# First cross-attention: turned scores of two key blocks at a time, kept in their banks by key differences

## Chip, cores and metric

The kernel runs on one core of a Trainium2 chip. The metric is the device time of one execution in microseconds (us), the median of several runs; smaller is better. Matmuls run on TensorE (PE in the profile, its weight loads on the row PEld), the other engines are VectorE (DVE), ScalarE (ACT), GpSimd (POOL) and SyncE (SP), which issues most DMAs. PSUM has eight banks of 128x512 float32 that matmuls write to; one bank holds one 512-column result.

## What is computed

The program is a two-layer decoder for 4 batches of 256 tokens and 256 channels. The change is inside the first layer's cross-attention alone. Its scores are 256 queries times 1601 keys for each of 16 heads and 4 batches; keys and values of a batch are the same 1601x64 array for all heads once the per-head matrices are folded into the queries:

```python
kv_r = _apply_rope(kv_c, sin_k[None], cos_k[None])
q_r = jnp.einsum('bshq,hqr->bhsr', q_big, W_qr)
k_r = jnp.einsum('bld,hdr->bhlr', kv_r, W_kr)
scores = jnp.einsum('bhsr,bhlr->bhsl', q_r, k_r)
attn = jax.nn.softmax(scores, axis=-1)
ctx_c = jnp.einsum('bhsl,bld->bhsd', attn, kv_r)
```

Before it stand the first layer's recurrent attention and the query products, after it the experts and the second layer; of these the change touches only what borders on the stage.

## The kernel before

The stage is a loop over 32 units (`UNITS = B * PAIRS`): a unit is one batch b and one pair p of heads. `QALL` holds the queries turned, split into a high part of reduced precision (fp32r) and the rest: for head h of the pair, rows 64h to 64h+63 hold the high part and the other 64 rows the low part. The keys of a batch lie turned in `KH` (high part, the same 64 rows twice, one above the other) and `KL` (low part). The 1601 keys make 13 blocks of 128, the last of 65.

A unit has four kinds of PE work. **Plain scores** (`plain_scores`, six per unit, and `plain_tail` for the last 65 keys): high parts only, queries on PSUM's partitions, two heads at once on the upper and lower 64 rows of the array, 2x512 columns into two banks. DVE takes their row maxima (`maxima`, L1620; `tail_maxima`, L1628; `all_maxima`, L1636), PE turns the four columns of maxima into rows (`turn_maxima`, L728), and DVE spreads these rows into rows 64 to 67 of `QM` (`maximum_rows`, L1644). **Turned scores** (`turned_scores`): keys on the partitions, for each of the 13 blocks one matmul `KH` with all 128 rows of `QALL` and one `KL` with `QM` (64 rows of high parts and the four maxima), 512 columns each, so that the bank holds score minus maximum. ACT writes its exponential into `PWS` (`weights`, L1277). **Context** (`context`): 13 blocks of weights times the values `KVR`, in float32, both heads side by side on the array's columns, into bank 7. **Weight sums** (`weight_sums`, of the unit before): POOL adds up the weights (`added_up`: five adds of 128x1024, L2075, one of 128x512, L2079, one of 65x512, L2082), PE sums over the partitions, DVE inverts the sums, multiplies the context and splits it (`normalised`, L1653 and L1657, `low_part`, L1663; `high_part` on ACT, L1288).

PSUM: banks 0 to 2 go round (`st_bank`) among turned blocks, tails, turned maxima, turned keys of the next batch and sums; banks 3 to 6 are two pairs for the plain scores (`plain_banks`). Plain scores run a unit ahead of their use. Every engine runs its own list in order; a `wait_ge` holds the engine's next instruction and all behind it. In 12 of the units PE also turns a quarter of the next batch's keys (`keys`, L684), ACT copies them out and DVE subtracts. All matmuls of the stage but the turns carry line L515, that of the helper `mm`.

The order of PE within a unit: the first six turned blocks, the tail of the next unit, two plain scores, the other seven blocks, two plain scores, the turn of the next maxima, keys if due, the sums of the unit before, the 13 context blocks, two plain scores.

Of the kernel before, what the change touches and what calls it, by code (L numbers as in the profile page):

```python
# [13 lines left out]
P = 128  # L14
# [13 lines left out]
HALF = 512  # L28
# [6 lines left out]
QW = 192  # L35
E0, E1 = 8, 16
# [50 lines left out]
def decoder(nc, x, ctx_512, L0_attn_Wk, L0_attn_Wv, L0_attn_Wr, L0_attn_Wo, L0_attn_time_decay, L0_attn_time_first,  # L87
# [5 lines left out]
    with ExitStack() as ctx:  # L93
# [75 lines left out]
        KH = [at("KH0", 65536, [P, L + 1], F32R), at("KH1", 78400, [P, L + 1], F32R)]  # L169
        KL = [at("KL0", 71968, [P, L + 1], F32R), at("KL1", 145152, [P, L + 1], F32R)]  # L170
        PWS = at("PWS", 104480, [P, 15 * HALF])
        PW = [PWS[:, 2 * HALF * c:2 * HALF * (c + 1)] for c in range(6)] + [PWS[:, 14 * HALF:15 * HALF]]
        ACC = PWS[:, 12 * HALF:14 * HALF]
        QM = [at(f"QM{i}", 135200 + 2048 * i, [P, HALF], F32R) for i in range(2)]
        WS = [at(f"WS{i}", 139296 + 2048 * i, [P, HALF]) for i in range(2)]
        pm = [at(f"pm{i}", 143392 + 128 * i, [P, 2, 2, 4]) for i in range(2)]
        nm = [at(f"nm{i}", 143456 + 32 * i, [P, 4]) for i in range(2)]
# [208 lines left out]
        kl_ready = sem("key_low_parts")  # L386
# [40 lines left out]
        CHUNKS = 7  # L427
        PLAINS = 6
        ADDS = 7
        FRONT, BACK = range(0, 6), range(6, LT)  # L430
# [12 lines left out]
        def keys_due(u):  # L443

            b, p = divmod(u, PAIRS)
            return (b + 1, p // 2) if p % 2 == 0 and b < B - 1 else None

        AHEAD = 4

        def plains_after(u):  # L450

            return [[n for n in range(PLAINS * (u + 1) + a, PLAINS * (u + 1) + z) if n < PLAINS * UNITS]
                    for a, z in ((4, 6), (6, 8), (8, 10))]

        ST_ITEMS = [("tail", 0), ("maxima", 0)]
        for u in range(UNITS):
            ST_ITEMS += [("block", LT * u + lt) for lt in (FRONT if u else range(LT))]
            ST_ITEMS += [("tail", u + 1)] if u + 1 < UNITS else []
            ST_ITEMS += [("block", LT * u + lt) for lt in (BACK if u else ())]
            ST_ITEMS += [("maxima", u + 1)] if u + 1 < UNITS else []  # L460
            ST_ITEMS += [("keys", *keys_due(u))] if keys_due(u) else []
# [4 lines left out]
        def st_bank(*item):  # L466

            n = ST_AT[item] % 3
            return PS[:, n * 512:(n + 1) * 512]

        def plain_banks(n):

            return PS[:, (3 + 2 * (n % 2)) * 512:(5 + 2 * (n % 2)) * 512]

        def st_freed(n):

            kind, *at_ = ST_ITEMS[n]
            return {"keys": lambda: (kl_ready, 4 * (at_[0] - 1) + at_[1] + 1), "maxima": lambda: (qm_ready, at_[0] + 1),
                    "block": lambda: (p_ready, at_[0] + 1), "tail": lambda: (tail_read, at_[0] + 1),
                    "sums": lambda: (norm_done, at_[0] + 1)}[kind]()  # L480
# [26 lines left out]
        def _(pe):  # L507
# [143 lines left out]
            def first_keys():  # L651

                pe.wait_ge(dup_ready, 2)
                for q in range(4):
                    ps = begin(("k", q), "dve")
# [3 lines left out]
                    last.then_inc(filled, 1)  # L659

            wait_ht(1)
            banks.start_at(4)
# [15 lines left out]
            def keys(b, q):  # L678

                pe.wait_ge(dup_ready, 2 * (b + 1))  # L680
                ps = st_begin("keys", b, q)
# [5 lines left out]
            def plain_scores(n):  # L687

                u, i = divmod(n, PLAINS)
# [4 lines left out]
                if n == 1:  # L694
                    pe.wait_ge(*banks.emptied(("q", PAIRS - 1, 0)))
                if n >= 2:
                    pe.wait_ge(nat_read, n - 1)
                if p == 0 and b > 0:
                    pe.wait_ge(kl_ready, 4 * (b - 1) + i % 3 + 1)
                for h in range(2):  # L700
                    st, k0 = i // 3, i % 3 * HALF
                    last = mm(plain_banks(n)[:, h * 512:(h + 1) * 512], QALL[h * D:(h + 1) * D, p, b, h, st * P:(st + 1) * P],
# [3 lines left out]
            def plain_tail(u):  # L706

                b, p = divmod(u, PAIRS)
                if u == 0:
                    pe.wait_ge(*banks.emptied(("q", PAIRS - 1, 1)))  # L710
                    pe.wait_ge(rows_set, 1)
                    for s in range(2):
                        pe.wait_ge(q_moved[s], 32 * PAIRS)
                ps = st_begin("tail", u)
                if p == 0 and b > 0:
                    pe.wait_ge(rows_set, 2)
                    pe.wait_ge(kl_ready, 4 * b)
                for h in range(2):
                    for st in range(2):
                        a = h * 256 + st * P  # L720
                        last = mm(ps[:, a:a + 66], QALL[:, p, b, h, st * P:(st + 1) * P], KH[b % 2][:, 3 * HALF:3 * HALF + 66])
                last.then_inc(tail_full, 1)

            def turn_maxima(u):

                pe.wait_ge(mx_ready, u + 1)
                ps = st_begin("maxima", u)
                nc.tensor.transpose(ps[0:4, 0:P], nm[u % 2][:, :], ident[:, :]).then_inc(mt_full, 1)  # L728

            def turned_scores(u, blocks):  # L730

                b, p = divmod(u, PAIRS)
                if blocks is FRONT:
                    pe.wait_ge(qh_moved[u % 2], 32 * (u // 2 + 1))
                    pe.wait_ge(qm_ready, u + 1)
                for lt in blocks:
                    w = P if lt < LT - 1 else LREST + 1
                    ps = st_begin("block", LT * u + lt)[0:w, :]
                    mm(ps, KH[b % 2][:, lt * P:lt * P + w], QALL[:, p, b, :, :], True, False)
# [1637 lines left out]
```

## Time and profile before

| | us |
|---|---|
| median of 3 runs (1345.43 to 1349.94) | 1347.24 |
| the profiled execution | 1343.5 |
| its span, first to last instruction | 1341.7 |
| PE busy in the span | 1241.2 (93%) |
| DVE, ACT, POOL busy | 890.9, 630.1, 821.2 |
| cross-attention loop, first plain score to last context (193.46 to 710.83) | 517.4 |

The span is read in stretches: the loop of 32 units lies between 193.46 and 710.83 us. A timeline row gives start, duration, engine, line, operation, output<-inputs, shape and count; durations of matmuls are modelled ends of pipelined instructions, so the step from one start to the next tells what a matmul costs, and the duration does not. In brackets stands how long the engine had been idle and what released it.

### The profile page before, as it was taken

The page shows a single profiled execution, that of the slowest core. Times are in us where ns is not written, and L with a number is a line of the kernel's source. Part 1 is how long each engine was busy: PE and PEld are TensorE (multiplying, and loading weights), DVE is VectorE, ACT ScalarE, POOL GpSimd, SP SyncE. Part 2 cuts the span into 40 slices and gives each one's busy share as a digit, 9 for nine tenths or more (in the row PEclk, how much of TensorE's full clock was granted, in tenths as well). Part 3 has the DMA queues.
Part 4 walks back from the last instruction along what each step waited for, and adds up shares of the span by engine and source line. Part 5 has one row for each costly group of instructions (what it writes and reads, how often), then busy time and mean ns, then how long its engine had stood idle before and what let it go on. Part 6 is the DMA issues. An engine that isn't in the chain of part 4 may idle for free.

```text
span 1341.7 us, 20371 instructions
## 1 busy us (share of the span) xinstructions
PE 1241.2 (93%) x7123; PEld 811.9 (61%) x7123; DVE 890.9 (66%) x1522; ACT 630.1 (47%) x1669; POOL 821.2 (61%) x747
## 2 busy tenths in 40 slices
PE   7999988999999999999999758998999998998992
PEld 4865545666666666666668644444777785557682
DVE  4789995777777777778865636766666213664643
ACT  3721123544445455444551514887766124882251
POOL 1267005999999999999993444888544002661354
PEclk9989998999999999999999787999999999999997
DMA  9501110000000000000005620000000105200273
GB/s 268 138 9 40 40 40 12 9 13 9 9 9 9 9 9 13 9 8 9 9 5 181 196 67 6 1 1 1 1 1 1 29 0 159 64 2 33 63 158 117
DMA packets 66172, 58.91 MB, mean 44 GB/s; under 512 B 19424, under 2 KB 62968, under 8 KB 65560
## 3 DMA queue, kind: packets, MB, share of 16 engines
q1 hardware_dynamic: 62952, 49.09, 13.1%
q0 software_dynamic: 3120, 8.52, 2.8%
q8 instruction: 58, 0.95, 0.3%
q14 instruction: 42, 0.34, 0.1%
HBM read 40.69 MB, written 8.52 MB: 37 GB/s over the span
## 4 chain that ended last, share of the span: by engine, by line
PE 78%; DVE 6%; ACT 6%; POOL 5%; issue 3%; DMA 2%; DVEq 0%; POOLq 0%; SPq 0%; ACTq 0%
PE PS L515 72%; PE PS L523 5%; ACT s_sc L1393 2%; POOL a_m L2132 2%; POOL a_m L2126 2%; DVE s_mx L1857 2%; ACT a_m L1347 1%; POOL e_yg L2180 1%; DVE pm L1620 1%; DVE HN L1495 1%; PE PS L728 0%; DVE stats L1485 0%; DMA f_xg<-token_rows,f_ids 0%; POOL s_sc L2147 0%; ACT PWS L1277 0%
## 5 line engine op out<-in xcount | busy, mean ns | idle before, releaser
L2075 POOL TENSOR_TENSOR PWS<-PWS 128x1024 f32<-128x1024 f32 x160 | 379.5, 2372 | 43.1 <-ACT PWS L1277 23.7
L1620 DVE TENSOR_REDUCE pm<-PS 128x2 f32<-128x1024 f32 x192 | 225.9, 1219 | 65.9 <-PE PS L515 65.2
L1277 ACT ACTIVATE PWS<-PS 128x512 f32<-128x512 f32 (+1 forms) x416 | 212.7, 600 | 76.7 <-PE PS L515 75.2
L515 PE MATMUL PS<-PWS,KVR 128*64 128x256 f32 (+1 forms) x1664 | 186.2, 380 | 0.0
L515 PE MATMUL PS<-QALL,KH 128*128 128x512 f32 (+1 forms) x416 | 181.7, 437 | 0.9 <-DVE QM L1644 0.9
L515 PE MATMUL PS<-QM,KL 68*128 68x512 f32 (+1 forms) x416 | 166.0, 399 | 0.0
L2147 POOL TENSOR_SCALAR s_sc<-s_sc,s_ri 128x128 f32<-128x128 f32 (+1 forms) x256 | 103.9, 425 | 92.4 <-DVE s_ri L1864 92.4
L515 PEld LDWEIGHTS PS<-PWS,KVR 128*64 128x64 f32 (+1 forms) x1664 | 122.0, 138 | 58.7 <-issue 1.1
L515 PEld LDWEIGHTS PS<-QALL,KH 128*128 128x128 f32 (+1 forms) x416 | 77.2, 186 | 77.1 <-ACT PWS L1277 57.4
L1393 ACT ACTIVATE s_sc<-PS,s_nb 128x128 f32<-128x128 f32 (+1 forms) x256 | 104.3, 432 | 4.5 <-DVE s_nb L1860 4.5
L1857 DVE TENSOR_REDUCE s_mx<-PS 128x2 f32<-128x512 f32 (+2 forms) x112 | 65.7, 611 | 45.5 <-PE PS L515 45.4
L515 PE MATMUL PS<-KH,QALL 64*128 64x512 f32 (+1 forms) x512 | 88.7, 406 | 6.9 <-DVE pm L1620 6.9
L515 PE MATMUL PS<-a_wT,HT 128*128 128x512 f32 x192 | 93.6, 621 | 0.7 <-issue 0.7
L1288 ACT ACTIVATE QALL<-CTX 128x256 fp32r<-128x256 f32 x32 | 13.3, 417 | 154.3 <-DVE CTX L1657 154.3
L515 PEld LDWEIGHTS PS<-QM,KL 68*128 68x128 f32 (+1 forms) x416 | 78.3, 188 | 5.8
L515 PEld LDWEIGHTS PS<-KH,QALL 64*128 64x128 f32 (+1 forms) x512 | 46.7, 187 | 43.4 <-issue 25.8
L2126 POOL TENSOR_TENSOR a_m<-a_m,a_m 128x512 f32<-128x512 f32 x40 | 50.8, 1270 | 29.6 <-DVE a_m L1834 29.6
L1516 DVE TENSOR_TENSOR X<-X,PS 128x256 f32<-128x256 f32 x40 | 16.7, 419 | 76.6 <-PE PS L515 76.6
L515 PE MATMUL PS<-z_HTh,z_w 128*128 128x512 f32 x192 | 65.7, 412 | 1.8 <-DVEq L502 1.8
L1262 ACT ACTIVATE QALL<-PS 64x512 fp32r<-64x512 f32 x32 | 18.9, 592 | 94.8 <-PE PS L515 94.4
L2175 POOL DMA_INDIRECT e_x<-token_rows,e_ids x31 | 29.4, 949 | 54.5 <-DVE e_ids L1954 44.5
L1653 DVE RECIPROCAL PS<-PS 128x256 f32<-128x256 f32 x32 | 55.9, 1747 | 6.6 <-PE PS L515 6.6
(333 smaller groups left out, 2487.3 us busy)
## 6 DMA issues: line engine op xcount, KB each, us to landing
QALL<-qlo SPq DMA_DIRECT2D x32, 128.0 KB, 2.4
QM<-QALL SPq DMA_DIRECT2D x64, 64.0 KB, 2.0
f_w<-in_L_ffn_w_dram SPq DMA_DIRECT2D x2, 2048.0 KB, 16.4
tile_results<-e_y SPq DMA_DIRECT2D x31, 128.0 KB, 2.5
a_nat<-in_L_attn_w_qkv_dram SPq DMA_DIRECT2D x1, 3072.0 KB, 12.7
x_wq<-in_L_xattn_Wq_dram SPq DMA_DIRECT2D x1, 2048.0 KB, 10.9
x_wo<-in_L_xattn_Wo_dram SPq DMA_DIRECT2D x2, 1024.0 KB, 7.3
a_wo<-in_L_attn_w_o_dram SPq DMA_DIRECT2D x1, 2048.0 KB, 17.2
```

The lines of the kernel that those rows point to most:

```text
L515: return nc.tensor.matmul(o, a, b, start=start, stop=stop, **kw)
L523: last = nc.tensor.transpose(ps[0:w, c:c + r], a, ident[0:r, 0:r])
L1277: nc.scalar.activation(PW[c][0:rows, j * HALF:(j + 1) * HALF], st_bank("block", LT * u + lt)[0:rows, :], ACT.Exp).then_inc(p_ready, 1)
L1393: ins = nc.scalar.activation(s_sc[:, k % 4, h, 0:nk], ps[:, j * nk:(j + 1) * nk], ACT.Exp, bias=s_nb[:, k % 3, h:h + 1], scale=scale, accu ...
L1620: V.tensor_reduce(pm[u % 2][:, :, i // 3, i % 3], src, AX, ALU.max).then_inc(nat_read, 1)
L1653: V.reciprocal(sums, sums).then_inc(inv_ready, 1)
L1857: ins = V.tensor_reduce(s_mx[:, k % 3, i * per:(i + 1) * per], banks.bank(key)[:, 0:per * nk].rearrange("p (h k) -> p h k", h=per), AX, AL ...
L2075: G.tensor_tensor(ACC[:, :], PW[0][:, :] if i == 0 else ACC[:, :], PW[i + 1][:, :], ALU.add).then_inc(acc_step, 1)
L2126: G.tensor_tensor(a_m1[:, n % 6, :], a_m1[:, n % 6, :], a_m2[:, n % 2, :], ALU.add).then_inc(m_sum, 1)
L2132: G.tensor_tensor(m1, m1, a_bt[:, i, s, :].unsqueeze(1).to_broadcast([P, 4, P]), ALU.add).then_inc(qk_ready, 1)
L2147: ins = G.tensor_scalar(s_sc[:, n % 4, h, 0:nk], s_sc[:, n % 4, h, 0:nk], s_ri[:, n % 4, h:h + 1], 1.0, ALU.mult, ALU.mult)
L2175: G.indirect_dma_start(e_x[:, j % 8, :], None, xs1, IndirectOffsetOnAxis(ap=e_ids[:, j:j + 1], axis=0)).then_inc(tile_back[j % 8], 16)
```

## The change

Turned scores are now taken for two key blocks at a time (`turned_pair`): block 2j on the upper 64 rows of the array, block 2j+1 on the lower 64, each into a bank of its own. So a unit has seven parts (`PARTS = 7`), six of two whole blocks and one of the last 65 keys. Because 64 rows hold only one part of a query, each product is made in steps: the key's high part with `QALL` (512 columns), with `QS`, a copy of the queries with halves swapped (512 columns), and the key's low part with each head's high part (256 columns each). The last part splits its two heads over the halves instead of two blocks.

The maxima are no longer added to every block. `max_rows` writes them at the start of a unit into the four banks 0 to 3 (part j uses banks 0 and 1 or 2 and 3), and each part adds onto what its banks hold. From part 2 on, the stationary operand is not the keys of a block but their difference to the block four earlier, so that the bank moves from one score to the next. These differences are made once per batch on POOL (`PD`, in `doubled`), turned, and split into `KDH` and `KDL`. `KH` stays for the plain scores, `KL` goes.

With this the banks are dealt out anew: one pair (4 and 5) for the plain scores instead of two, one bank (6) for turned maxima, keys and sums in turn instead of three that go round, banks 2 and 3 also for the tails. ACT takes two banks in one exponential of 128x1024, seven per unit for thirteen. The context comes in three parts between the others, and plain scores are spread singly. POOL's add of 128x512 goes; PE's weight sums have two steps of accumulation for one. `normalised` writes into bank 6 and `high_part` and `low_part` read it there, one unit later. Keys are due in 18 units instead of 12: four of each batch turn whole keys (ACT copies), two turn differences (ACT copies, DVE subtracts). SP copies 128 KB twice per unit into `QS`, for 64 KB twice into `QM`.

The core of the diff, PE's side first:

```diff
+        ST_BANK = PS[:, 6 * 512:7 * 512]
+        PLAIN_BANKS = PS[:, 4 * 512:6 * 512]
+        TAIL_BANKS = PS[:, 2 * 512:4 * 512]
...
+        def pair_banks(j):
+            return PS[:, 2 * (j % 2) * 512:2 * (j % 2 + 1) * 512]
...
             def st_begin(*item):
                 n = ST_AT[item]
-                if n >= 3:
-                    pe.wait_ge(*st_freed(n - 3))
-                return st_bank(*item)
+                if n >= 1:
+                    pe.wait_ge(*st_freed(n - 1))
+                return ST_BANK
...
-                if n >= 2:
-                    pe.wait_ge(nat_read, n - 1)
+                else:
+                    pe.wait_ge(nat_read, n)
...
+            def max_rows(u, j):
+                pe.wait_ge(qm_ready, u + 1)
+                if u > 0:
+                    pe.wait_ge(p_ready, PARTS * (u - 1) + PARTS - j)
+                if j == 1:
+                    pe.wait_ge(tail_read, min(u + 2, UNITS))
+                for s in range(2):
+                    rows = slice(s * D, (s + 1) * D)
+                    mm(pair_banks(j)[:, s * 512:(s + 1) * 512], ones_r[rows, :], MX[rows, :], True, False,
+                       skip_group_check=True)
+
+            def turned_pair(u, j):
...
+                if j >= 2:
+                    pe.wait_ge(p_ready, PARTS * u + j - 1)
...
+                    for q in (QALL[:, p, b, :, :], QS[u % 2]):
+                        for s, rows in enumerate(halves):
+                            mm(both[:, s * 512:(s + 1) * 512], KDH[b % 2][rows, cols], q[rows, :, :], False, False,
+                               skip_group_check=True)
+                    for h in range(2):
+                        for s, rows in enumerate(halves):
+                            q = QALL[rows, p, b, h, :] if s == h else QS[u % 2][rows, h, :]
+                            last = mm(both[:, s * 512 + h * T:s * 512 + (h + 1) * T], KDL[b % 2][rows, cols], q, False, True,
+                                      skip_group_check=True)
...
             for u in range(UNITS):
+                spots = plains_of(u)
+                plain_scores(spots[0])
                 if u + 1 < UNITS:
                     plain_tail(u + 1)
+                max_rows(u, 0)
+                turned_pair(u, 0)
+                max_rows(u, 1)
+                turned_pair(u, 1)
+                plain_scores(spots[1])
+                context(u, (0, 1))
+                plain_scores(spots[2])
+                turned_pair(u, 2)
+                turned_pair(u, 3)
+                plain_scores(spots[3])
+                context(u, (2, 3))
+                plain_scores(spots[4])
+                turned_pair(u, 4)
+                turned_pair(u, 5)
+                plain_scores(spots[5])
+                turned_pair(u, 6)
                 if u + 1 < UNITS:
                     turn_maxima(u + 1)
                 if keys_due(u):
                     keys(*keys_due(u))
                 if u >= 1:
                     weight_sums(u - 1)
-                context(u, range(LT))
+                context(u, (4, 5, 6))
```

DVE's list of a unit and ACT's exponentials:

```diff
             for u in range(UNITS):
+                spots = plains_of(u)
                 if u + 1 < UNITS:
                     tail_maxima(u + 1)
+                for n in spots[0:4]:
                     maxima(n)
                 if u + 1 < UNITS:
                     all_maxima(u + 1)
+                if u >= 2:
+                    low_part(u - 2)
+                for n in spots[4:6]:
                     maxima(n)
                 if u + 1 < UNITS:
                     maximum_rows(u + 1)
                 if keys_due(u):
                     keys(*keys_due(u))
...
+                if j < PARTS - 1:
+                    nc.scalar.activation(PW[j], pair_banks(j), ACT.Exp).then_inc(p_ready, 1)
```

## Rows read from the trace of the kernel before

**Rows 1.** Two whole units: us, busy us (instructions) of each engine, PEclk, DMA.

```profile
457.39:473.36 15.97, 15.97 (x106) 9.95 (x104) 11.32 (x14) 7.81 (x16) 14.98 (x8) 1.00 0.05 11
473.36:488.90 15.54, 15.54 (x103) 9.55 (x101) 12.62 (x13) 7.64 (x16) 14.67 (x8) 1.00 0.03 8
```

**Rows 2.** Chain of waits, 440 to 500 us: start, us, what carried the end.

```profile
456.98 15.32 PE PS L515 x98
```

**Rows 3.** Timeline of PE, 455 to 480 us.

```profile
456.91 0.65 PE L515 MATMUL PS<-WS,ones 128*64 128x256 f32 x4
457.39 5.78 PE L515 MATMUL PS<-PWS,KVR 128*64 128x256 f32 x52
463.11 0.73 PE L515 MATMUL PS<-KH,QALL 64*128 64x512 f32 x4
463.77 0.50 PE L515 MATMUL PS<-QALL,KH 128*128 128x512 f32 x1
464.11 0.39 PE L515 MATMUL PS<-QM,KL 68*128 68x512 f32 x1
...
468.54 0.40 PE L515 MATMUL PS<-QALL,KH 128*128 128x512 f32 x1
...
469.47 0.50 PE L515 MATMUL PS<-QALL,KH 128*128 128x512 f32 x1
...
472.34 0.60 PE L684 MATMUL PS<-ident,DUP 128*128 128x128 f32 x4
472.87 0.65 PE L515 MATMUL PS<-WS,ones 128*64 128x256 f32 x4
```

**Rows 4.** Timeline of PE's weight loads, 463.0 to 463.3 us.

```profile
463.11 0.30 PEld L515 LDWEIGHTS PS<-KH,QALL 64*128 64x128 f32 x4 [0.39 <-issue]
```

**Rows 5.** Timeline of PE, 712.0 to 712.45 us: 256 columns each, after the loop.

```profile
712.08 0.28 PE L515 MATMUL PS<-UL,QALL 128*128 128x256 f32 x1
...
712.43 0.28 PE L515 MATMUL PS<-UL,QALL 128*128 128x256 f32 x1
```

**Rows 6.** Timeline of POOL, 465 to 482 us.

```profile
467.79 12.44 POOL L2075 TENSOR_TENSOR PWS<-PWS 128x1024 f32<-128x1024 f32 x5
480.31 1.35 POOL L2079 TENSOR_TENSOR WS<-PWS 128x512 f32<-128x512 f32 x1
481.74 1.29 POOL L2082 TENSOR_TENSOR WS<-WS,PWS 65x512 f32<-65x512 f32 x1
```

**Rows 7.** Timeline of DVE, 455 to 480 us.

```profile
463.65 2.36 DVE L1620 TENSOR_REDUCE pm<-PS 128x2 f32<-128x1024 f32 x2 [0.96 <-PE PS L515]
467.41 0.43 DVE L1628 TENSOR_REDUCE pm<-PS 128x4 f32<-128x260 f32 x1 [1.40 <-PE PS L515]
...
470.24 0.17 DVE L1636 TENSOR_REDUCE nm<-pm 128x4 f32<-128x16 f32 x1
...
474.50 0.68 DVE L1644 TENSOR_TENSOR QM<-PS,ident 4x512 fp32r<-4x512 f32 x1
```

**Rows 8.** DVE's groups by form, 190 to 715 us: busy, mean ns, idle before.

```profile
L1663 DVE TENSOR_TENSOR CTXL<-CTX,QALL 128x256 fp32r<-128x256 f32 x31 | 45.4, 1465 | 15.0 <-ACT QALL L1288 15.0
...
L1657 DVE TENSOR_TENSOR CTX<-CTX,PS 128x256 f32<-128x256 f32 x31 | 13.0, 421 | 1.1
```

**Rows 9.** ACT's groups by form, whole span: busy, mean ns, idle before.

```profile
L1277 ACT ACTIVATE PWS<-PS 128x512 f32<-128x512 f32 x384 | 197.5, 601 | 76.7 <-PE PS L515 75.2 <-POOL WS L2079 1.0 <-issue 0.4
...
L1288 ACT ACTIVATE QALL<-CTX 128x256 fp32r<-128x256 f32 x32 | 13.3, 417 | 154.3 <-DVE CTX L1657 154.3
L1283 ACT ACTIVATE CTX<-PS 128x256 f32<-128x256 f32 x32 | 12.3, 384 | 35.5 <-PE PS L515 35.5
```

**Rows 10.** Timeline of ACT, 455 to 480 us.

```profile
464.62 3.08 ACT L1277 ACTIVATE PWS<-PS 128x512 f32<-128x512 f32 x6 [1.01 <-PE PS L515]
```

**Rows 11.** Timeline of PE's weight loads, 684 to 685 us: a load that waits.

```profile
684.70 0.19 PEld L515 LDWEIGHTS PS<-QALL,KH 128*128 128x128 f32 x1 [0.27 <-ACT PWS L1277]
```

**Rows 12.** DMA issues of the page: KB each, us to landing.

```profile
QALL<-qlo SPq DMA_DIRECT2D x32, 128.0 KB, 2.4
```

More of the change, by code:

```diff
@@ L35 @@
 QW = 192
+PARTS = 7
 E0, E1 = 8, 16
@@ L659, in first_keys, with turn_pairs @@
                     last.then_inc(filled, 1)
+                pe.wait_ge(dup_ready, 5)
+                for i in range(2):
+                    turn_pairs(begin(("paired", i), "dve"), 0, i).then_inc(filled, 1)
+            def turn_pairs(ps, b, i):
+                for n, j in enumerate(range(4 * i, min(4 * i + 4, PARTS))):
+                    w = P if j < PARTS - 1 else LREST
+                    last = nc.tensor.transpose(ps[:, n * P:n * P + w], PD[b][0:w, j, :], ident[0:w, 0:w])
+                return last
             wait_ht(1)
-            banks.start_at(4)
+            banks.start_at(2)
             z_jobs(0)
@@ new lines, in context @@
+            def context(u, chunks):
+                b = u // PAIRS
+                if chunks[0] == 0:
+                    pe.wait_ge(*((ctx_read, u) if u else banks.emptied(("q", PAIRS - 1, 1))))
+                for c in chunks:
+                    pe.wait_ge(p_ready, PARTS * u + c + 1)
+                    for j, lt in enumerate(range(2 * c, min(2 * c + 2, LT))):
+                        w = P if lt < LT - 1 else LREST
+                        for h in range(2):
+                            last = mm(CTX_BANK[h * D:(h + 1) * D, 0:T], KVR[0:w, b, lt, :],
+                                      PW[c][0:w, j * HALF + h * T:j * HALF + (h + 1) * T], lt == 0, lt == LT - 1)
+                    last.then_inc(ctx_part, 1)
@@ L760, in weight_sums @@
                 ps = st_begin("sums", u)
-                for h in range(2):
-                    last = mm(ps[h * D:(h + 1) * D, 0:T], ones[:, 0:D], WS[u % 2][:, h * T:(h + 1) * T])
+                for k in range(2):
+                    for h in range(2):
+                        last = mm(ps[h * D:(h + 1) * D, 0:T], ones[:, 0:D], ACC[u % 2][:, k * HALF + h * T:k * HALF + (h + 1) * T],
+                                  k == 0, k == 1)
                 last.then_inc(sum_full, 1)
@@ L1293, in _ @@
             for u in range(UNITS):
-                weights(u, FRONT)
-                weights(u, BACK)
+                for j in range(PARTS):
+                    weights(u, j)
+                    if j == 0 and u >= 2:
+                        high_part(u - 2)
                 if keys_due(u):
                     keys(*keys_due(u))
-                if u >= 1:
-                    high_part(u - 1)
                 if 0 <= u - SPLIT_FROM < PAIRS:
```

321 lines of the change are left out of this document (165 added, 156 removed).

## Prediction, made before the changed kernel ran

> **What bounds the kernel now.** Read two whole units in stretches first [rows 1]: one with a key step takes 15.97 us, one without 15.54. PE is busy for all of both, POOL for 14.98 and 14.67, DVE for 11.32 and 12.62, ACT for under 8, at a granted clock of 1.00 (2.4 GHz). The chain of waits [rows 2] stays on PE's matmuls for a unit at a time. So PE's own list sets the pace: nothing it asks for is late. POOL comes next: five adds take 12.52 from the first start to the start of the small add, which is 1.43 from the next [rows 6]; with two small adds that is 15.38, only 0.16 under PE. Twenty units without and twelve with keys make 20 x 15.54 + 12 x 15.97 = 502.4 us. The sum below is made against the profiled execution, 1343.5; the median of the runs, 1347.2, lies 3.7 above it, and I add that at the end. About 0.3% (4 us) is what a measurement of this kernel can tell from no change.
>
> **Prices on PE.** A matmul of 512 columns on the full array costs 0.232: four steps lie between 468.54 and 469.47 [rows 3]. Two matmuls on the upper and lower 64 rows run together: the plain scores do that now, and four of them, two pairs, take 0.66 from 463.11 to 463.77 [rows 3]. Two steps of 0.232 are 0.46; the other 0.20 is the price of changing the array's mode: about 0.1 of idling, and a first weight load that nothing hides (the first matmul of a run lasts 0.50, later ones 0.39). That the second pair's weights load beside the first pair shows in the four loads: they begin at 463.11 and have ended by 463.41 [rows 4]. So a pair costs what one full matmul costs, 0.232. For 256 columns the nearest rows are those after the loop, three steps in 0.35 or 0.117 each [rows 5]; I take 0.118 for a pair, with 0.232 as the upper end (weights that cost as much as in a 512-column step). A turn or a tail piece costs 0.11 to 0.13 (four turns in 0.53 with the change of mode, [rows 3]); two heads' context for a block 0.432 (13 in 5.72 with the change), the sums 0.48 with a change of mode of 0.05, so 0.43 for their two steps.
>
> **PE's work per unit after the change, waits apart.** Context 13 x 0.432 = 5.62. Plain scores 6 x 0.232 = 1.39. Tail, two pairs, 0.22. Maxima rows 2 x 0.232 = 0.46. Six parts of two 512- and two 256-column pairs, 6 x 0.70 = 4.20. The last part 3 x 0.118 = 0.35. Turn of maxima 0.11. Sums, now two steps of accumulation, 0.86. Changes of mode: three back to rows and one to the turn at 0.21, three to columns at 0.15: 1.29. Together 14.50, against 15.54: a gain of 1.04 per unit, of which the turned scores alone give 26 x 0.232 = 6.03 less 5.01. Key steps cost 0.43 in 18 units for 12 before.
>
> **What falls off the path.** POOL: five adds and one small one, 12.52 + 1.43 = 13.95, below PE. The differences for three batches (a copy of 256, subtractions of 512 and 128 columns, about 2.1 by the 1.35 of a 512-column add) fit into POOL's slack, and cost 2.1 each without it. ACT: six exponentials of 1024 columns, about 8 per unit in all. SP: two transfers of 128 KB land in about 2.4 [rows 12], queued a whole unit ahead; without that cover they would cost 2.4 per unit. DVE's total falls to about 11.3.
>
> **The new waits.** A walk through one unit in PE's order decides. Zero is the end of the previous context. Prices: from the issue of a first plain pair to DVE's start 0.54 (463.11 to 463.65, [rows 3, 7]), of which 0.11 is the weight load, 0.22 the stream, 0.22 the way; a reduction 1.18 to 1.22 (two in 2.36), I take 1.19; tail maxima 0.43, column maxima 0.17 and now twice, maxima rows 0.69 [rows 7]. From matmul to ACT likewise 0.22 to 0.28 (464.11 + 0.23 to 464.62, [rows 3, 10]). An exponential of 1024 columns is not in the trace: 512 take 0.601 and 256 columns 0.384 [rows 9], so 0.434 more, 1.0; ends are 0.87 (column time alone) and 1.2 (two of 512). ACT can start the next one 0.09 earlier (six in 3.08, [rows 10]). An engine's answer reaches PE 0.05 later.
> - PE: plain A at 0.21, tail, maxima rows, part 0 to 1.60, part 1 to 2.53. Plain B needs A reduced, because the pair of banks is now single: DVE has done the tail by 1.31 and A by 2.50; wait 0.13.
> - ACT: exponential 0 from 1.82 to 2.82, then the high part moved in between (0.42, [rows 9]), exponential 1 to 4.06. PE is at its context at 3.91: wait 0.25.
> - Plain C, parts 2 and 3, plain D at 6.86: C is reduced at 6.87, and the weights load exposed: wait 0.17. Context of parts 2 and 3 waits 0.07 and 0.05 for exponentials that end at 7.38 and 8.29.
> - Plain E at 9.47, parts 4 and 5, plain F: wait 0.17, issued at 11.16. Part 6 adds onto the banks of part 4, whose exponential ends at 11.62: wait 0.28, done at 12.13, then the turn of the maxima.
> - The sums use the same bank 6 as that turn, and wait until DVE has made the maxima rows from it. DVE takes its list in order: reduction of F from 11.72 to 12.91, rows to 13.60. PE could have started at 12.46 and starts at 13.65: **wait 1.19**. Behind the sums stand five context blocks and the whole next unit. Before, three banks went round and this answer had a context of 5.7 to hide in.
> - Sums and five blocks: the unit ends at 16.73, that is 14.50 and 2.3 of waits.
>
> In a key unit bank 6 is passed on once more: the keys wait for the maxima rows, the sums for ACT's copy of the keys (0.60): 1.41 more, 18.14, in 12 units. In the 6 that turn differences DVE's subtraction follows (0.69 and 0.05): 18.88. POOL and DVE have slack against such periods. `low_part` reads PSUM now: nearest is the other product with one PSUM operand, 0.42, and not the 1.47 with both operands in SBUF [rows 8]; were it 1.47, plain F would be later by half a us, 17 us in all.
>
> Sum: 14 x 16.73 + 12 x 18.14 + 6 x 18.88 = 565.2, against 502.4: **62.8 us more**. At the edges six first plain scores now follow one another at 1.8 rather than 1.19 (+3), seven more turns cost 0.8, unit 0 has no sums and unit 31 no maxima to wait for (-3); I count them as nothing, within 5. So 1343.5 + 62.8 = 1406.3, and by the median 1410.
>
> The bounds: four exponentials of the unit lie on its path, so 1.2 instead of 1.0 costs 0.8 per unit, 26 us, and 0.87 gives back 12. The 256-column pairs at 0.232 add 15 x 0.114 = 1.7 per unit, half of it inside waits: 27. The low part adds 17. Any one of the upper ends with the edges gives about 1441, the lower end 1388 to 1393.
>
> **Rivals.**
> 1. *PE goes past the held instruction* (faster). Place: the sums at bank 6. If only the waiting matmul were held and the five context blocks behind it ran, 2.2 of work would cover the 1.19, and the other waits would fill likewise. Price: -1.04 x 32 + 6 x 0.43 = -30.7, so 1316. It decides as soon as the waits of a unit stay under the gain of 1.04. For it: POOL's 13.95 would allow it. Against: a weight load that waits for ACT today leaves PEld idle for 0.27 although work for other banks stands behind it [rows 11]. 5%.
> 2. *Weights of a row half load only when that half is free.* Then nearly every pair bears a load of 0.107: some 26 per unit that are not exposed anyway, 2.8 x 32 = 89 more: 1499. The four loads of [rows 4] speak against it: two begin while the first pair runs. 5%. The Trainium skill, page "TensorE: Matmul & The Clock Gate", section "The mechanism", states that a weight load overlaps running matmuls only when its row group differs; by that rule this rival would be the forecast. The trace differs here: [rows 4] has loads for both row groups beside matmuls on both.
> 3. *The halves do not run together when they add onto banks* (the change doesn't do what it says). The plain scores start their banks anew, so no row shows it. Fourteen pairs of 512 and fifteen of 256 would double: 5.0 per unit, 161 us less at most 35 of waits hidden: about 1550. Against: matmuls that add cost the same 0.23 as those that start a bank [rows 3]. 2%.
> 4. *Half of the waits are covered* by something I can't see: they are 3.0 per unit on average, so 48 less: 1362. 5%. If two thirds were covered, no change: 3%.
>
> **How the numbers follow.** The forecast, waits as walked, 1410, has 80%, with its range 1388 to 1441. Rivals 2 and 3 (7%) lie above, 1 and 4 (13%) below, so that range leaves 20% out and stands. Faster by over 0.3%: 5%. Within: 3%. Slower: 92%.
>
> **What would show it.** In the trace after: PE idle before the sums, about 1.2 in plain units and twice that with keys, released by DVE's maxima rows or by ACT's copy of the keys; unit periods near 16.7, 18.1 and 18.9; pairs 0.232 apart and 0.118 for 256 columns; exponentials near 1.0; POOL idle for some 2.8 per unit, where it now idles for under one. If the periods lie under 15.7, the walk is wrong; if PE is busy throughout and slower, a price is.

## The result, and the profile after

The changed kernel takes 1424.46 us (median, 1421.91 to 1425.0); the kernel before took 1346.34 beside it. The ratio is 1.058 (95% interval 1.054 to 1.063): slower by 78 us, where 63 were forecast. The profiled execution took 1421.91 with a span of 1419.5. Its 78 us all lie in the loop of 32 units: from the start of the first plain score to the start of the last context matmul it takes 597.1 us now for 517.0 (the 517.4 of the table ahead goes to that matmul's end), 80 us more, and what lies around the loop is 2 us shorter. Loops are read between these two starts from here on.

From the page after: busy us, share and instructions of the engines, and the granted clock in 40 slices.

```profile
PE 1254.6 (88%) x8303; PEld 839.5 (59%) x8303; DVE 862.9 (61%) x1547; ACT 618.3 (44%) x1485; POOL 783.1 (55%) x731
PEclk9999979999999999999999978899999999999997
```

PE is busy for 88% now, 93% before. Its 1254.6 us are 13 more than before, and the other engines are busy for less: work did not grow by 78 us, something waits. Three units after, in stretches (us, busy us and instructions of PE, PEld, DVE, ACT, POOL, then PEclk, DMA share, GB/s): one without keys, then two with keys. They answer [rows 1].

```profile
342.27:359.17 16.90, 15.49 (x135) 10.30 (x136) 11.06 (x14) 6.96 (x10) 15.63 (x10) 1.00 0.08 17
359.18:379.16 19.98, 17.78 (x140) 11.70 (x140) 11.06 (x14) 7.55 (x11) 13.08 (x6) 0.91 0.06 14
379.16:397.46 18.30, 16.09 (x140) 10.71 (x140) 11.06 (x14) 7.55 (x11) 13.09 (x6) 1.00 0.07 15
```

The second and the third do the same work, and differ by 1.68 us and by the granted clock. Rows of PE's timeline of the unit without keys, from its third plain block on (start, duration, operation, output<-inputs, shape, count; in brackets the idle time and who ended it); it answers [rows 3]:

```profile
344.39 0.50 PE L513 MATMUL PS<-KH,QALL 64*128 64x512 f32 x2
344.72 0.39 PE L513 MATMUL PS<-QALL,KDH 64*128 64x512 f32 x2
344.95 0.40 PE L513 MATMUL PS<-QS,KDH 64*128 64x512 f32 x2
345.19 0.28 PE L513 MATMUL PS<-QALL,KDL 64*128 64x256 f32 x1
...
345.43 0.40 PE L513 MATMUL PS<-QALL,KDH 64*128 64x512 f32 x2
...
351.63 0.30 PE L745 MATMUL PS<-ident,nm 128*68 128x128 f32 x1
353.05 1.08 PE L513 MATMUL PS<-PWS,ones 128*64 128x256 f32 x8 [1.12 <-DVE MX L1715]
353.94 2.36 PE L513 MATMUL PS<-PWS,KVR 128*64 128x256 f32 x20
```

The reader sees the forecast's main wait: PE idles for 1.12 us between the turn of the maxima and the sums, until DVE has made the maxima rows (forecast 1.19). DVE's timeline shows why; it makes them only after the reduction of the sixth plain block:

```profile
351.09 1.23 DVE L1688 TENSOR_REDUCE pm<-PS 128x2 f32<-128x1024 f32 x1 [0.60 <-PE PS L513]
352.23 0.68 DVE L1715 TENSOR_TENSOR MX<-PS,spread 68x512 fp32r<-68x512 f32 x1
```

In a key unit bank 6 is passed on twice. PE's timeline in two key units, the first at full clock, the second (from 408.23) not; behind them the stretch from each unit's sums on:

```profile
389.93 0.63 PE L695 MATMUL PS<-ident,DUP 128*128 128x128 f32 x4 [1.14 <-DVE MX L1715]
391.34 1.08 PE L513 MATMUL PS<-PWS,ones 128*64 128x256 f32 x8 [0.78 <-ACT KH L1328]
...
408.23 0.63 PE L695 MATMUL PS<-ident,DUP 128*128 128x128 f32 x4 [1.14 <-DVE MX L1715]
409.64 1.83 PE L513 MATMUL PS<-ACC,ones 128*64 128x256 f32 x8 [0.78 <-ACT KH L1328]
```

```profile
391.34:394.50 3.16, 3.16 (x28) 2.27 (x28) 2.00 (x2) 0.00 (x0) 3.08 (x2) 1.00 0.00 0
409.60:412.90 3.30, 3.26 (x17) 2.32 (x19) 1.40 (x1) 0.00 (x0) 3.22 (x2) 0.53 0.00 0
```

The waits are the same. But in the second unit the sums take 1.83 instead of 1.08, at a granted clock of 0.53, that is at 1.2 GHz for nearly all of the stretch, in which PE gets through 17 matmuls where the first unit has 28. The record of the granted clock holds 11 such stretches of 3.41 us in the loop after its beginning, every one in a unit with keys; before, the loop had none after its beginning. That is the part of the loss that the forecast did not have.

### The profile page after: what moved, and what is told of

Same layout as the page of the kernel before. It is cut to its first block, busy times and chain, and to the rows that moved or that the text cites. A ratio compares the mean times of both kernels' runs of the same rounds, so it can differ in the third digit from the quotient of the medians.

```text
span 1419.5 us, 22602 instructions
## 1 busy us (share of the span) xinstructions
PE 1254.6 (88%) x8303; PEld 839.5 (59%) x8303; DVE 862.9 (61%) x1547; ACT 618.3 (44%) x1485; POOL 783.1 (55%) x731
## 4 chain that ended last, share of the span: by engine, by line
PE 71%; ACT 8%; DVE 7%; issue 6%; POOL 5%; DMA 2%; POOLq 0%; ACTq 0%; SPq 0%; DVEq 0%
PE PS L513 66%; PE PS L521 4%; ACT PWS L1339 3%; ACT s_sc L1458 2%; POOL a_m L2216 2%; DVE MX L1715 2%; POOL a_m L2210 1%; DVE s_mx L1930 1%; ACT a_m L1412 1%; POOL e_yg L2264 1%; DVE pm L1688 1%; DVE HN L1560 1%; PE PS L695 0%; DVE stats L1550 0%; DMA f_xg<-token_rows,f_ids 0%
## 5 line engine op out<-in xcount | busy, mean ns | idle before, releaser
L1339 ACT ACTIVATE PWS<-PS 128x1024 f32<-128x1024 f32 x192 | 189.9, 1024 | 209.2 <-PE PS L513 209.0
L2163 POOL TENSOR_TENSOR PWS<-PWS 128x1024 f32<-128x1024 f32 x80 | 189.2, 2365 | 82.9 <-ACT PWS L1339 75.8
L2163 POOL TENSOR_TENSOR ACC<-ACC,PWS 128x1024 f32<-128x1024 f32 x64 | 151.2, 2362 | 21.5 <-ACT PWS L1339 14.4
L513 PE MATMUL PS<-QALL,KDH 64*128 64x512 f32 (+1 forms) x448 | 87.2, 384 | 3.5 <-ACT PWS L1339 1.3
L513 PE MATMUL PS<-QALL,KDL 64*128 64x256 f32 (+1 forms) x448 | 85.9, 277 | 0.0
L513 PE MATMUL PS<-QS,KDH 64*128 64x512 f32 (+1 forms) x448 | 85.6, 376 | 0.0
L513 PEld LDWEIGHTS PS<-KH,QALL 64*128 64x128 f32 x512 | 46.8, 189 | 58.5 <-issue 35.8
L513 PEld LDWEIGHTS PS<-QALL,KDL 64*128 64x128 f32 (+1 forms) x448 | 75.4, 178 | 8.3
L513 PEld LDWEIGHTS PS<-QS,KDL 64*128 64x128 f32 x384 | 71.0, 185 | 8.1
L513 PE MATMUL PS<-QS,KDL 64*128 64x256 f32 x384 | 74.8, 278 | 0.0
```

The source lines that it names most:

```text
L513: return nc.tensor.matmul(o, a, b, start=start, stop=stop, **kw)
L1339: nc.scalar.activation(PW[j], pair_banks(j), ACT.Exp).then_inc(p_ready, 1)
L2163: G.tensor_tensor(acc, PW[0][:, :] if i == 0 else acc, PW[i + 1][:, :], ALU.add).then_inc(acc_step, 1)
```

## Experiments

Theory A: the waits around the shared bank 6 set the loss. Theory C: the half-clock stretches come from the two stalls of a key unit, close to one another. Rival B: PE's own work on pairs and halves sets the period, and the waits are only where spare time shows.

| kernel | us | ratio to before (95%) |
|---|---|---|
| changed | 1424.46 | 1.058 (1.054 to 1.063) |
| maxima turned early | 1372.73 | 1.021 (1.018 to 1.024) |
| context first | 1408.04 | 1.049 (1.045 to 1.053) |
| no low parts | 1424.22 | 1.059 (1.055 to 1.062) |
| maxima and keys early | 1346.76 | 1.0025 (1.0007 to 1.0042) |
| stalls filled | 1407.81 | 1.046 (1.042 to 1.051) |
| before, with the bank passed on | 1497.03 | 1.113 (1.108 to 1.119) |
| reordered | 1338.02 | 0.9947 (0.9920 to 0.9975) |

### Maxima turned early

```diff
                 turned_pair(u, 5)
+                if u + 1 < UNITS:
+                    turn_maxima(u + 1)
                 plain_scores(spots[5])
                 turned_pair(u, 6)
-                if u + 1 < UNITS:
-                    turn_maxima(u + 1)
...
-                for n in spots[4:6]:
-                    maxima(n)
+                maxima(spots[4])
                 if u + 1 < UNITS:
                     maximum_rows(u + 1)
+                maxima(spots[5])
```

> The changed kernel with one edit: the next unit's maxima are turned one place earlier (after part 5's scores, ahead of the sixth plain block, and not after part 6), and VectorE writes the rows of maxima ahead of that block's reduction, not behind it. The shared bank and its pass-on stay. Theory A (waits for the bank passed on set the loss): the wait of 1.12 us before the sums on VectorE's rows of maxima is gone, in the 19 units without keys the period falls from 16.90 to 15.4, in the 12 key units from about 18.1 and 18.9 at full clock to 16.8 and 17.5 (the wait for ScalarE's key copy stays); the time falls by some 35 us to about 1388. Theory C (the half-clock stretches of key units come from two stalls close to one another): with one of the two gone the stretches go too, 11 x 1.65 = 18 us more, about 1370. Rival B (TensorE's own work on the pairs, with its changes of mode, sets the period, and the wait is only where spare time shows): the wait turns up elsewhere, above all at the next unit's first plain block, since the sixth reduction starts 0.7 us later; period over 16.6, time 1415 or more.

Measured 1372.73, 52 us less than the changed kernel. PE's timeline of a unit without keys and of one with keys:

```profile
339.92 0.30 PE L745 MATMUL PS<-ident,nm 128*68 128x128 f32 x1
340.15 0.50 PE L513 MATMUL PS<-KH,QALL 64*128 64x512 f32 x2
...
341.09 1.08 PE L513 MATMUL PS<-PWS,ones 128*64 128x256 f32 x8
...
356.67 0.63 PE L695 MATMUL PS<-ident,DUP 128*128 128x128 f32 x4
358.07 1.08 PE L513 MATMUL PS<-ACC,ones 128*64 128x256 f32 x8 [0.78 <-ACT KH L1328]
```

The sums no longer wait in the one, the keys no longer in the other, and nothing as long appears elsewhere: units without keys take 15.55 to 15.61 (16.90), and 16.12 in five of the last, where DVE also splits the output weights; whole-key units take 16.97 (18.30 at full clock). One half-clock stretch is left, in a unit that turns differences (19.35, its like 17.72). Rival B is out. The loop takes 545.4, 51.7 less. Against the run with the stalls filled (below; 580.4, with no such stretch) it is 35.0 shorter, and its one stretch costs 1.6: so 36.6 us go to the waits, and the other 15 to ten stretches.

### Context first

```diff
+                context(u, (4, 5, 6))
                 if keys_due(u):
                     keys(*keys_due(u))
                 if u >= 1:
                     weight_sums(u - 1)
-                context(u, (4, 5, 6))
```

> The changed kernel with the last context part (parts 4 to 6) issued ahead of the key blocks and the sums, not behind them. Theory A in its simple form: the context's 1.1 us of work fills the wait of 1.12 us before the sums, 31 units x 1.1 = 34 us, about 1390. Theory A followed through the walk: the sums then end 1.1 us later, VectorE's reciprocal (1.8 us) and product (0.4 us) start that much later, and its reductions of the next unit's tail and first block behind them; the wait turns up at the next unit's first pairs; no gain, 1418 to 1430. Rival B (TensorE's own work sets the period): no change either; the two differ in the profile: by the walk TensorE's idle time is about the same and stands at other places, by B no place waits for VectorE for more than 0.3 us.

Measured 1408.04: neither 1390 nor no change. The waits moved, as walked. The sums of a key unit still wait for the copy, and DVE comes late to the next unit's tail, so that the maxima rows for part 1, which share its banks, wait. PE's and DVE's timelines of one such place:

```profile
385.71 1.08 PE L513 MATMUL PS<-PWS,ones 128*64 128x256 f32 x8 [0.78 <-ACT KH L1328]
...
389.54 0.49 PE L513 MATMUL PS<-MX,ones_r 64*128 64x512 f32 x2 [1.17 <-ACT PWS L1339]
```

```profile
386.83 1.77 DVE L1724 RECIPROCAL PS<-PS 128x256 f32<-128x256 f32 x1 [3.81 <-PE PS L513]
388.63 0.43 DVE L1727 TENSOR_TENSOR PS<-CTX,PS 128x256 f32<-128x256 f32 x1
388.97 0.42 DVE L1697 TENSOR_REDUCE pm<-PS 128x4 f32<-128x260 f32 x1
```

The row names ACT, but the instruction waits for DVE too, and it starts 0.15 after the tail's reduction ends at 389.39. So the periods are the same at full clock: 16.87 for 16.90, whole-key units 18.44 for 18.30. What came back, 16 us, is the clock alone: no half-clock stretch is left in the loop after its beginning (loop 580.2). The two stalls are still 0.78 and 1.17 long, but 2.66 us of work lie between them (385.71 to 388.37) where 0.63 us lay before, and the clock stays up.

### Stalls filled

```diff
+            def useless(u, times):
+
+                for _ in range(times):
+                    mm(PS[:, 7 * 512 + 256:8 * 512], ones_r[:, :], KH[u // PAIRS % 2][:, 0:256], skip_group_check=True)
...
                 if keys_due(u):
+                    useless(u, 6)
                     keys(*keys_due(u))
+                    useless(u, 4)
```

> The changed kernel with ten useless matmuls of 256 columns (their results go nowhere) in each of the 18 units with keys: six ahead of the keys, where TensorE waits 1.14 us for VectorE, and four ahead of the sums, where it waits 0.78 us or more for the keys' copies. Nothing is moved and no wait is taken away; TensorE only stands idle for less of it. Theory C (the half-clock stretches of 3.41 us in 11 of the 18 key units come from these two stalls close to one another, 1.65 us lost in each): the stretches go, all key units take what they take at full clock (about 18.2, and 18.8 with differences), the time falls by 15 to 18 us to about 1407. Rival (the clock falls for a reason that has nothing to do with the stalls, such as the sum of work): the stretches stay, and the time stays at 1424 or grows by the useless work that is not covered (up to 18 x 0.3 = 5 us).

(The useless matmuls write to the unused half of the bank in which the context is being added up. This run does not keep the context right and is read for its time alone.) Measured 1407.81, 16.7 less, with ten matmuls more in 18 units. PE's timeline in a key unit, and that unit as a stretch:

```profile
364.13 0.95 PE L513 MATMUL PS<-KH,ones_r 128*128 128x256 f32 x6
365.51 0.63 PE L695 MATMUL PS<-ident,DUP 128*128 128x128 f32 x4 [0.43 <-DVE MX L1722]
365.90 0.72 PE L513 MATMUL PS<-KH,ones_r 128*128 128x256 f32 x4
366.92 1.08 PE L513 MATMUL PS<-ACC,ones 128*64 128x256 f32 x8 [0.30 <-ACT KH L1335]
```

```profile
354.70:373.00 18.30, 17.28 (x149) 11.89 (x149) 11.06 (x14) 7.55 (x11) 13.12 (x6) 1.00 0.07 15
```

The keys still start when DVE's rows are there, and the sums when the copy is; only PE's idling in between fell from 1.14 and 0.78 to 0.43 and 0.30. All stretches at half clock after the loop's beginning are gone, and every whole-key unit takes 18.1 to 18.3 (17.6 with the short last block), as the undisturbed ones did in the changed kernel. This run shortened the stalls and added work; the run with the context first kept the work and moved the two stalls apart, at 0.78 and 1.17 hardly shorter or longer, with the same effect. Together they settle theory C: idling twice so close together, not the amount of work, brought the clock down in these units, for 16.7 us. The loop takes 580.4 here, 63.4 more than the 517.0 of before.

### No low parts

```diff
-                            mm(both[:, s * 512:(s + 1) * 512], KDH[b % 2][rows, cols], q[rows, :, :], False, False,
-                               skip_group_check=True)
-                    for h in range(2):
-                        for s, rows in enumerate(halves):
-                            q = QALL[rows, p, b, h, :] if s == h else QS[u % 2][rows, h, :]
-                            last = mm(both[:, s * 512 + h * T:s * 512 + (h + 1) * T], KDL[b % 2][rows, cols], q, False, True,
+                            last = mm(both[:, s * 512:(s + 1) * 512], KDH[b % 2][rows, cols], q[rows, :, :], False, True,
                                       skip_group_check=True)
...
-                    for k, own in ((KDH, True), (KDH, False), (KDL, True)):
+                    for k, own in ((KDH, True), (KDH, False)):
```

> The changed kernel without the products of the low parts of the key differences (part of the computation is left out): 12 pairs of 256-column matmuls at 0.118 us in parts 0 to 5 and one pair in part 6, 1.53 us of TensorE's time in each of 32 units. Rival B (TensorE's own work sets the period): all 49 us come back, about 1375. Theory A (the waits for VectorE and ScalarE around the shared bank and the exponentials set it): TensorE arrives earlier at the same waits; by the walk 11 us come back, about 1413, and TensorE's idle time before part 2 to part 6 and before the sums is longer by the rest.

Measured 1424.22: 49 us of PE's work left out, nothing gained. PE's timeline in a unit without keys, that unit as a stretch, and another without keys:

```profile
505.07 0.49 PE L513 MATMUL PS<-KH,QALL 64*128 64x512 f32 x2 [0.39 <-DVE pm L1683]
...
507.57 1.08 PE L513 MATMUL PS<-PWS,ones 128*64 128x256 f32 x8 [1.48 <-DVE MX L1710]
```

```profile
497.10:513.50 16.40, 14.05 (x111) 8.24 (x111) 11.05 (x13) 6.91 (x11) 15.71 (x10) 1.00 0.08 17
349.10:367.30 18.20, 15.86 (x113) 9.36 (x111) 11.05 (x13) 7.02 (x11) 15.78 (x10) 0.91 0.07 16
```

At full clock the unit falls from 16.90 to 16.46, 0.44 of the 1.53 taken out; the rest stands in longer waits (1.48 before the sums for 1.12, and 0.39 before the fourth and again before the sixth plain block). That is theory A's 11 us, nearly: 32 x 0.44 = 14. They went to the clock: half-clock stretches come in units without keys too, 16 in all for 11, nine of them of 6.83 us. Rival B's 49 us are out.

### Before, with the bank passed on

```diff
                 if n >= 3:
                     pe.wait_ge(*st_freed(n - 3))
+                if item[0] in ("keys", "sums"):
+                    pe.wait_ge(*st_freed(n - 1))
                 return st_bank(*item)
```

> The kernel before with only its ring of three banks passed on as the changed kernel passes on its one: keys and sums wait until the item directly before them has been read out, not the one three before. No pairs, no halves, no key differences. Theory A (the pass-on alone costs most of what the change loses): the sums wait for VectorE's rows of maxima behind two reductions, 2.3 us in each of 31 units, and in the 12 units with keys the keys wait for the rows, and the sums for the keys' copy and low parts, 1 to 2 us more; by the walk some 100 us, about 1445, with half-clock stretches on top. Rival B (the pairs and halves of the change cost it, not the pass-on): under 20 us slower, about 1360, because GpSimd's adds set the period of 15.5 us and hide what TensorE waits.

Measured 1497.03, 153 us more than before by this alone. PE's timeline in a unit without keys and in the next, with keys, and three units as a stretch:

```profile
413.40 0.65 PE L515 MATMUL PS<-WS,ones 128*64 128x256 f32 x4 [2.82 <-DVE QM L1646]
...
431.91 1.05 PE L686 MATMUL PS<-ident,DUP 128*128 128x128 f32 x4 [2.83 <-DVE QM L1646]
434.46 1.12 PE L515 MATMUL PS<-WS,ones 128*64 128x256 f32 x4 [1.50 <-DVE KL L1612]
```

```profile
393.10:455.50 62.40, 52.43 (x304) 33.31 (x302) 34.24 (x37) 22.97 (x46) 40.68 (x21) 0.91 0.03 7
```

Rival B had said under 20. The waits come to 29 x 2.82, 9 x 1.50 and five shorter ones, 99 us, where the walk had 100; the other 54 go with 25 half-clock stretches in the loop after its beginning, 109 us at half clock in all. Of these, 14 lie in units without keys, where PE idles once, for 2.82 us. No turned pair and no key difference is in this kernel. POOL's adds, which had nearly the same period as PE [rows 1, 6], hide nothing of it: POOL is busy for 40.68 of 62.40.

### Maxima and keys early

```diff
                 plain_scores(spots[3])
+                if keys_due(u):
+                    keys(*keys_due(u))
                 context(u, (2, 3))
...
                     weights(u, j)
+                    if j == 3 and keys_due(u):
+                        keys(*keys_due(u))
```

(On top of the first experiment; the order in which the bank is passed on follows, and the high and low parts are moved as the expectation says.)

> The changed kernel with the turned maxima one place earlier and the key blocks in the middle of the unit (after the fourth plain block, ScalarE's copy of them after exponential 3, VectorE's low parts of the differences after the unit's maxima), the high part of the context one exponential later, VectorE's low part of it after the third reduction, and the low part of the output weights after the second. The one shared bank stays, now passed on where nobody waits. Theory A: all waits of the bank go; by the walk the units take 15.1 (plain) and 15.6 us (key), the loop 512 us as against 579 of the walk of the changed kernel: 66 us less, about 1358; with theory C (no stalls close together, no half-clock stretches) 18 us less again, about 1340, just under the kernel before. Rival B (pairs, halves and mode changes cost TensorE more than the windows show): no better than the run with the maxima alone earlier, 1390 or more.

Measured 1346.76, 78 us less than the changed kernel, level with before but for 0.25%; the expectation's 1340 was met by the profiled execution, the shortest of ten, at 1340.08. A unit without keys and one with keys as stretches:

```profile
430.00:445.30 15.30, 15.06 (x135) 10.30 (x136) 11.03 (x14) 6.93 (x10) 12.90 (x7) 1.00 0.08 18
460.60:476.40 15.80, 15.58 (x141) 10.91 (x142) 11.13 (x14) 7.53 (x11) 15.07 (x8) 1.00 0.08 18
```

PE is busy for 15.06 of 15.30 and 15.58 of 15.80; periods are 15.33 and 15.72 (walk 15.1 and 15.6), the loop 514.1 (walk 512), and no half-clock stretch is left in it after its beginning. There is still one bank, passed on just as often. It is only asked for where its last user has long read it.

### Reordered

```diff
-                plain_scores(spots[0])
                 if u + 1 < UNITS:
                     plain_tail(u + 1)
                 max_rows(u, 0)
+                plain_scores(spots[0])
                 turned_pair(u, 0)
...
                 plain_scores(spots[1])
-                context(u, (0, 1))
-                plain_scores(spots[2])
+                if keys_due(u):
+                    keys(*keys_due(u))
                 turned_pair(u, 2)
                 turned_pair(u, 3)
+                plain_scores(spots[2])
+                context(u, (0, 1, 2))
                 plain_scores(spots[3])
-                context(u, (2, 3))
-                plain_scores(spots[4])
                 turned_pair(u, 4)
                 turned_pair(u, 5)
-                plain_scores(spots[5])
-                turned_pair(u, 6)
+                plain_scores(spots[4])
                 if u + 1 < UNITS:
                     turn_maxima(u + 1)
-                if keys_due(u):
-                    keys(*keys_due(u))
+                context(u, (3,))
+                turned_pair(u, 6)
+                plain_scores(spots[5])
```

> The run with maxima and keys early, with TensorE's order in a unit changed once more: tail and maxima rows ahead of the first plain block, the keys after the second, the context in parts 0 to 2, 3 and 4 to 6, plain blocks between the pairs where VectorE has just read the last one out; the high part of the context ahead of exponential 0 and its low part after the first reduction. In that run TensorE's idle time in a unit is under 0.5 us, so there is little left to wait for. By the walk the units with keys stay at 15.7 us, plain units come to 15.25, the last eight from 15.6 to about 15.3; 5 to 8 us less than that run: 1339 to 1342, ratio to the kernel before 0.996 to 0.999. If the changes of mode cost more than the walk counts, or GpSimd's adds (13.95 us and their starts) now set the period: no change, 1347.

Measured 1338.02, ratio 0.9947 (0.9920 to 0.9975): half a per cent below the kernel before, a little more than forecast. Units take 15.17 without keys and 15.4 with whole keys, for 15.54 and 15.97 before. A stretch of one unit's length:

```profile
428.00:443.30 15.30, 15.18 (x139) 10.40 (x137) 11.12 (x14) 7.26 (x11) 13.60 (x7) 1.00 0.08 18
```

The loop takes 503.2, 14 less than before. The medians show 6 of these 14; in the profiled execution what follows the loop is longer (638.9 for 631.2). The trace tells where. The same 300 matmuls of the second layer, which the change does not touch, as stretches of the kernel before and of this run:

```profile
1105.10:1156.10 51.00, 45.27 (x300) 26.71 (x300) 24.25 (x74) 28.04 (x106) 18.46 (x43) 0.97 0.38 105
1090.10:1150.30 60.20, 56.03 (x300) 31.52 (x301) 24.72 (x74) 28.04 (x106) 18.43 (x42) 0.77 0.33 89
```

They take 9.2 us longer here, at a granted clock of 0.77 for 0.97; the execution with the stalls filled had the same there. What brings the clock down there is not shown. So the new structure has a gain of its own once its order leaves PE waiting for little, though not the 31 us of rival 1's sum.

## Why the prediction was right, and where it was not

The sign and the range held; 14.5 us were missing, and the runs say where.

**The walk's waits.** The idle time before the sums measured 1.12 for 1.19; what a key step adds measured 18.30 - 16.90 = 1.40 for 1.41, 0.63 of turns and 0.78 of waiting. Units without keys take 16.90 for 16.73; whole-key units at full clock 18.30 for 18.14 (17.6 for the three with the short block); units with differences, with the stalls filled, 19.03 and 18.51 for 18.88. With the clock held up the loop costs 63.4 more, where the sum said 62.8. Two small sums of the prediction do not come out as written: 14.50 of work and 2.31 of waits make 16.81 and not 16.73, and an exponential of 0.87 would give back 4 x 0.13 x 32 = 16.6 and not 12; both are inside its bounds.

**The term that was mis-sized: the clock.** The walk priced every unit at the granted 1.00 of [rows 1]. 11 of 18 key units had 3.41 us at half, which cost 597.1 - 580.4 = 16.7 us by the kernel with filled stalls. The forecast had the two stalls beside one another in its own walk, and did not ask what they do to the clock. They raised the loss by a quarter. That the result lay inside the range all the same is luck: its bounds were set for exponentials, pairs and edges, and none for the clock. The Trainium skill, page "TensorE: Matmul & The Clock Gate", section "A second HAM failure mode: psum-queue depth-cycling", tells of a kernel in which frequent short idles between groups of matmuls make the clock go to and fro between its levels; the trace after agrees, at 1.14 and 0.78 us of idling.

**Work and waits, one by one.** PE's work was put at 14.50 per unit and the waits at 2.3. Busy time does not tell them apart: matmuls that start 0.23 apart are drawn 0.40 long, so short waits vanish in them, in the 15.06 of 15.30 of the run with maxima and keys early too. Steps from start to start do tell. A plain block and the context behind it, in the changed kernel and in the reordered one:

```profile
346.21 0.51 PE L513 MATMUL PS<-KH,QALL 64*128 64x512 f32 x2
346.79 2.00 PE L513 MATMUL PS<-PWS,KVR 128*64 128x256 f32 x16
...
322.70 0.41 PE L513 MATMUL PS<-KH,QALL 64*128 64x512 f32 x2
323.04 2.81 PE L513 MATMUL PS<-PWS,KVR 128*64 128x256 f32 x24
```

The step is 0.58 in one and 0.34 in the other, so the changed kernel waits 0.24 here. Read so, against the shortest step of the same kind in these runs, the wait before the sums is 1.42 - 0.23 = 1.19 (351.63 to 353.05 above, 339.92 to 340.15 in the first experiment; walk 1.19), and the small waits of a unit without keys come to 1.1 to 1.3 (walk 1.12). That leaves 14.4 to 14.6 of work, an estimate from these steps, where the forecast had 14.50. Both terms of the unit came out as forecast, to 0.2.

**Prices.** Groups of the loop after, by form (busy, mean ns, idle before and its cause), beside [rows 8, 9]:

```profile
L1339 ACT ACTIVATE PWS<-PS 128x1024 f32<-128x1024 f32 x192 | 189.9, 1024 | 209.2 <-PE PS L513 209.0
L1733 DVE TENSOR_TENSOR CTXL<-PS,QALL 128x256 fp32r<-128x256 f32 x30 | 12.4, 414 | 1.8 <-ACT QALL L1352 1.8
L1328 ACT ACTIVATE KH<-PS 128x512 fp32r<-128x512 f32 x9 | 5.4, 597 | 11.4 <-PE PS L695 11.4
```

The exponential of 1024 columns takes 1.02 (forecast 1.0, ends 0.87 and 1.2), the low part from PSUM 0.41 (0.42, upper end 1.47), the copy of the keys 0.60. Pairs of 512 are 0.23 apart (344.72 to 344.95 to 345.19), two pairs of 256 take 0.24 (345.19 to 345.43): 0.118 as taken.

**Rivals.** 1 (PE goes past the held instruction): the rows above show the sums held with the context behind them idle; out. 3 (halves don't run together when they add): a pair that adds costs 0.23; out. 4 (half of the waits covered): the waits at bank 6 are there in full, and the small ones add up to the walk's sum; out. 2 (weights of a half load only when it is free): PE and its loads in one timeline of the changed kernel:

```profile
377.01 0.39 PE L513 MATMUL PS<-QALL,KDH 64*128 64x512 f32 x2
377.01 0.19 PEld L513 LDWEIGHTS PS<-QS,KDH 64*128 64x128 f32 x2
377.23 0.40 PE L513 MATMUL PS<-QS,KDH 64*128 64x512 f32 x2
```

The next pair's two loads, one for each half, begin with the running pair and end before it; the pairs are 0.22 apart. Out. By the rule that rival 2 cites from the Trainium skill, page "TensorE: Matmul & The Clock Gate", section "The mechanism", these loads could not have run beside a pair that holds both row groups; the rows do not bear that out.

**What would show it.** Idle before the sums by DVE's rows and ACT's copy: as said. POOL's slack: it is busy for 783.1 against 821.2 and waits for exponentials. "Busy throughout and slower" did not happen, and the run without the low parts shows how little PE's work counted.

**Left open.** Of the whole-key units the second quarter of each batch keeps its clock (18.06 to 18.32) with the same two stalls as the third, which lost it each time. No run tells what saves it. The fourth quarter, whose short block makes the second stall 0.41 for 0.78, kept its clock in all three batches; the units with differences, with second stalls of 1.15 and 1.50, lost it in all six.

## What to carry to other kernels

A buffer that goes from user to user cost nothing by itself here: its price is the distance between one user's last read and the next one's start, in the list of the engine that reads. Put the hand-over where that reader's list is short, and move the asking to where the answer is old; here moving the maxima's turn and their rows by one place each gave back 52 of 78 us, and moving the keys and the splitting around them nearly all of the rest. And when a walk leaves two stalls near one another on TensorE, look at the granted clock before trusting the sum.

## What the hardware showed

Idle times of 1.14 and 0.78 us, with 0.63 us of turns between, were followed by a granted clock of 0.53 over 3.3 us; in 11 of 18 key units two stalls of this kind, the second of 0.78 to 1.50, brought a half-clock stretch of 3.41 us, 1.4 to 1.7 us lost each time. With 0.43 and 0.30 idle at the same places, or with 2.66 us of work between the stalls, it stayed at 1.00. In the kernel before with its bank passed on, a single stall of 2.82 us brought such a stretch in 14 of 18 units without keys. And leaving work out can cost clock: without the low parts PE had 14.05 busy of 16.40, with longer stalls, and lost the clock even in units without keys.
